# Splitting and turning the normalised attention output: GpSimd and DMA transposes in place of TensorE, ScalarE and VectorE

## What is computed

```python
x = x + tanh(g_xattn) * xattn(layernorm(x), ctx, Wq, Wk, Wv, Wo, bo)
x = x + tanh(g_ffn) * ffn(layernorm(x), gate_w, w_gate, w_up, w_down)

def xattn(x, context, Wq, Wk, Wv, Wo, bo):   # 16 heads of 16 channels
    q, k, v = x @ Wq.T, context @ Wk.T, context @ Wv.T          # split into heads
    scores = where(causal, einsum('bhqd,bhkd->bhqk', q, k) * 0.25, -inf)
    y = einsum('bhqk,bhkd->bhqd', softmax(scores), v)           # heads joined again
    return y @ Wo.T + bo

def ffn(x, ...):      # 8 experts, each takes the 128 tokens of a batch with the highest affinity
    affinity = softmax(x @ gate_w.T); gating, idx = top_k(affinity.T, 128)
    h = silu(x[idx] @ w_gate.T) * (x[idx] @ w_up.T)
    return scatter_add(idx, gating * (h @ w_down.T))
```

## Time and profile before

| | before |
|---|---|
| time of three runs, median (lowest to highest) | 2008.08 us (2006.38 to 2014.46) |
| the profiled execution: its own time; its span | 2008.71 us; 2006.9 us |
| busy share of the span: TensorE, VectorE, ScalarE, GpSimd | 92%, 56%, 45%, 35% |
| mean granted TensorE clock | 0.973 |
| attention, as a stretch of the trace | up to about 926 us |
| one body of attention in its steady part | 52.77 us |
| in such a body: TensorE, VectorE, ScalarE, GpSimd busy | 51.27, 42.32, 31.18, 22.55 us |

### The profile page before, as it was taken

The page is one execution under the profiler, slowest core; times in us unless marked ns, Lnnn a source line. Parts: engine busy times, 40 slices in busy tenths (PEclk is TensorE's granted clock), DMA queues, the critical chain, the costliest instruction groups (busy, mean ns, idle before and its releaser), DMA issues.

```text
span 2006.9 us, 41634 instructions
## 1 busy us (share of the span) xinstructions
PE 1847.0 (92%) x13800; PEld 1091.3 (54%) x13800; DVE 1122.4 (56%) x2745; ACT 898.1 (45%) x1716; POOL 709.5 (35%) x636
## 2 busy tenths in 40 slices
PE   3799999999999999992599999999999999999997
PEld 1455555555555555551256556565555656566565
DVE  3667787788887778766543443434333433434332
ACT  1355555555556555562243343433333333433332
POOL 4234444444444444223324233332424233342322
PEclk9799999999999999996799999999999999999999
DMA  4655565555555655526456454664545646444322
GB/s 128 147 143 144 162 166 154 155 149 161 156 161 161 167 158 163 132 82 154 132 103 125 81 98 85 115 122 85 99 81 95 122 74 120 94 73 90 58 28 26
DMA packets 378619, 238.32 MB, mean 119 GB/s; under 512 B 260600, under 2 KB 360064, under 8 KB 378496
## 3 DMA queue, kind: packets, MB, share of 16 engines
q1 hardware_dynamic: 353920, 203.14, 41.0%
q0 software_dynamic: 24576, 33.57, 10.6%
HBM read 118.63 MB, written 58.72 MB: 88 GB/s over the span
## 4 chain that ended last, share of the span: by engine, by line
PE 48%; DVE 2%; DMA 2%; issue 1%; POOL 0%; ACT 0%; DVEq 0%; POOLq 0%
PE bank L1037 11%; PE bank L1038 10%; PE bank L1039 10%; PE bank L1055 5%; PE bank L1053 5%; PE bank L1054 5%; DMA out<-y,row_now 1%; DVE top_at L1106 1%; DVE work L1109 1%; DVE top L1104 1%; POOL out L997 0%; DVE h L1144 0%; DMA tokT<-rows 0%; ACT y L1091 0%; POOL rows L989 0%
## 5 line engine op out<-in xcount | busy, mean ns | idle before, releaser
L558 ACT ACTIVATE prob<-bank 128x512 f32<-128x512 f32 x640 | 372.5, 597 | 221.6 <-PE bank L448 210.4
L997 POOL DMA_INDIRECT out<-y,row_now x128 | 201.6, 1575 | 661.4 <-ACT y L1091 637.1
L1144 DVE TENSOR_TENSOR h<-bank,silu 128x512 f32<-128x512 f32 x256 | 176.3, 689 | 341.4 <-PE bank L1039 340.4
L645 DVE CUSTOM_DVE_ANT_0 masked<-bank,causal 128x384 f32<-128x384 f32 (+1 forms) x512 | 299.3, 617 | 44.9 <-PE bank L428 44.1
L1083 ACT ACTIVATE h<-h 128x512 bf16<-128x512 f32 x256 | 161.1, 629 | 348.7 <-DVE h L1144 348.7
L428 PE MATMUL bank<-ks,qs 96*128 96x128 bf16 (+3 forms) x1024 | 277.8, 307 | 29.9 <-DMA ks<-k_parts 25.8
L1053 PE MATMUL bank<-downT,h 128*128 128x256 bf16 x1024 | 279.1, 273 | 0.0
L1054 PE MATMUL bank<-downT,h 128*128 128x256 bf16 x1024 | 279.1, 273 | 0.0
L1055 PE MATMUL bank<-downT,h 128*128 128x256 bf16 x1024 | 279.1, 273 | 0.0
L1147 DVE TENSOR_TENSOR h<-h 128x512 bf16<-128x512 f32 x256 | 177.2, 692 | 179.5 <-ACT h L1083 179.5
L446 PE MATMUL bank<-qs,ks 98*128 98x512 bf16 (+3 forms) x1024 | 268.4, 301 | 3.0 <-DMA qs<-m_sb 2.2
(11 more groups left out here) (144 smaller groups left out, 2784.0 us busy)
## 6 DMA issues: line engine op xcount, KB each, us to landing
qs<-q_parts SPq DMA_DIRECT2D x384, 64.0 KB, 2.7
ks<-k_parts SPq DMA_DIRECT2D x384, 64.0 KB, 2.7
q_parts<-q_sb SPq DMA_DIRECT2D x32, 384.0 KB, 3.1
k_parts<-k_sb SPq DMA_DIRECT2D x32, 384.0 KB, 3.2
x_t<-in_x SPq DMA_DIRECT2D x16, 512.0 KB, 4.1
ctx_t<-in_ctx SPq DMA_DIRECT2D x16, 512.0 KB, 4.9
res_t<-in_x SPq DMA_DIRECT2D x16, 512.0 KB, 5.6
out<-x SPq DMA_DIRECT2D x16, 512.0 KB, 3.0
```

The lines of the kernel that those rows point to most:

```text
L558: nc.scalar.activation(prob[:, gr % 2, h0:h0 + nh, POFF[tiles[0]]:POFF[tiles[0]] + w], sc_bank[SC_BANK[k]][:, 0:nh * w].rearrange("p (h w) ...
L645: nc.vector.tensor_tensor_reduce(masked[:, k % 2, 0:w], max_bank[max_at(gr, k)][:, 0:w], causal[:, T - w:T], 1.0, LOWEST, ALU.add, ALU.max ...
L997: nc.gpsimd.indirect_dma_start(out_rows, bass.IndirectOffsetOnAxis(ap=row_now[:, par, CHUNK * c + s:CHUNK * c + s + 1], axis=0), y[:, c % ...
```

## The change

`yb` and `yb+` go. Two new pieces take their place. `ysplit` (GpSimd) splits one half of `yq` into hi and lo in token layout, in the new tensor `y_nat`, with two instructions, at g1 k3 (half 0) and g3 k3 (half 1). `yturn` (SyncE) turns that half with one DMA transpose of 128x1024 bfloat16 into `ynT`, whose layout changes, at g1 k6 (half 0, first in its unit) and g3 k6 (half 1, ahead of `stack(b+1, 0)`). `o` waits for the transposes' semaphore. The job list has 20 entries a body instead of 22, so the alternation of banks is counted anew: `mt(b-1, 3)` (L469, g0 k4), which followed `yt(b-1, 0)` in one bank, now follows `v(b, 1)` of the body before.

```diff
         0: {...
-            2: [("yt+", b - 1, 0), ("yb", b - 2, 1), ("xsplit", b + 1, 1)],
-            3: [("pv", b - 1, 1, 2), ("mrow", b - 1, 3), ("yb+", b - 2, 1)],
+            2: [("yt+", b - 1, 0), ("xsplit", b + 1, 1)],
+            3: [("pv", b - 1, 1, 2), ("mrow", b - 1, 3)],
...
         1: {1: [("mt", b, 0)], 2: [("yt+", b - 1, 1)],
-            3: [("pv", b - 1, 2, 0), ("mt+", b, 0), ("ln2", b - 2, 0)],
+            3: [("pv", b - 1, 2, 0), ("mt+", b, 0), ("ln2", b - 2, 0), ("ysplit", b - 1, 0)],
...
-            6: [("q", b + 1, 1, 0), ("q", b + 1, 1, 1), ("q+", b + 1, 1)],
+            6: [("yturn", b - 1, 0), ("q", b + 1, 1, 0), ("q", b + 1, 1, 1), ("q+", b + 1, 1)],
...
         2: {...
-            3: [("yt", b - 1, 2), ("yb", b - 1, 0), ("yb+", b - 1, 0), ("k+", b + 1, 0)],
+            3: [("yt", b - 1, 2), ("k+", b + 1, 0)],
...
         3: {0: [("kstore", b + 1)], 1: [("mt", b, 2)],
-            2: [("mrow", b, 2), ("mt+", b, 2), ("yt", b - 1, 3), ("yt+", b - 1, 3)], 3: [("ll+", b - 2)],
+            2: [("mrow", b, 2), ("mt+", b, 2), ("yt", b - 1, 3), ("yt+", b - 1, 3)], 3: [("ll+", b - 2), ("ysplit", b - 1, 1)],
...
-            5: [("ln1", b + 2, 0)], 6: [("stack", b + 1, 0), ("lt", b - 2), ("lt+", b - 2), ("pv", b, 0, 1)],
+            5: [("ln1", b + 2, 0)], 6: [("yturn", b - 1, 1), ("stack", b + 1, 0), ("lt", b - 2), ("lt+", b - 2), ("pv", b, 0, 1)],
...
-JOBS_A_BATCH = {"yt": 4, "yb": 2, "o": 2, "mt": 4, "q": 2, "k": 2, "xt": 2, "ll": 1, "lt": 1, "v": 2}
+JOBS_A_BATCH = {"yt": 4, "o": 2, "mt": 4, "q": 2, "k": 2, "xt": 2, "ll": 1, "lt": 1, "v": 2}
...
-    ynT = sb(ctx, "ynT", [P, 2, NH2, T], BF16)
+    y_nat = sb(ctx, "y_nat", [P, NH2, 2, NT, P], BF16)
+    ynT = sb(ctx, "ynT", [P, NH2, 2, NT, P], BF16)
...
+                elif kind == "yturn":
+                    half = p[2]
+                    hold(split_lo["y"], count(b, 2, half + 1))
+
+                    hold(filled["o"], count(b, 2, 0))
+                    sp.dma_start_transpose(ynT[:, half, :, :, :].rearrange("p r i t -> p (r i) t"),
+                                           y_nat[:, half, :, :, :].rearrange("p r i d -> p (r i d)"))\
+                        .then_inc(flipped["y"], 16)
...
-                            wait(pe, read["yb"], count(b, 2, 2))
+                            wait(pe, flipped["y"], count(b, 32, 32))
...
-                        src = cT[:, rs, i, c, :] if kind == "v" else ynT[:, rs, c, i * P:(i + 1) * P]
+                        src = cT[:, rs, i, c, :] if kind == "v" else ynT[:, c, rs, i, :]
...
-                    wait(dve, filled["yb"], count(b, 2, gr // 2 - 1))
+                    wait(dve, split_lo["y"], count(b, 2, gr // 2 - 1))
...
+                elif kind == "ysplit":
+                    half = p[2]
+                    wait(pool, read["yt"], count(b, GROUPS, 2 * half + 2))
+
+                    wait_apart(pool, flipped["y"], count(b, 32, 16 * half - 16), passed["pool"])
+                    src = yq[:, :, half * P:(half + 1) * P]
+                    nc.gpsimd.tensor_copy(y_nat[:, half, 0, :, :], src).then_inc(split_hi["y"], 1)
+                    wait(pool, split_hi["y"], count(b, 2, half + 1))
+                    nc.gpsimd.tensor_tensor(out=y_nat[:, half, 1, :, :], in0=src, in1=y_nat[:, half, 0, :, :],
+                                            op=ALU.subtract).then_inc(split_lo["y"], 1)
```

More of the change, by code:

```diff
@@ L256, in attention @@
     read = {n: sem(f"{n}_read") for n in JOBS_A_BATCH}
-    hi_done = {n: sem(f"{n}_hi_done") for n in ("q", "k", "mt", "yb")}
+    hi_done = {n: sem(f"{n}_hi_done") for n in ("q", "k", "mt")}
     rest_split = sem("rest_split")
-    split_hi = {n: sem(f"{n}_hi_split") for n in ("x", "c")}
-    split_lo = {n: sem(f"{n}_lo_split") for n in ("x", "c")}
-    flipped = {n: sem(f"{n}_flipped") for n in ("x", "c")}
+    split_hi = {n: sem(f"{n}_hi_split") for n in ("x", "c", "y")}
+    split_lo = {n: sem(f"{n}_lo_split") for n in ("x", "c", "y")}
+    flipped = {n: sem(f"{n}_flipped") for n in ("x", "c", "y")}
     max_filled, max_read = sem("max_filled"), sem("max_read")
@@ L475, in piece @@
                     last.then_inc(filled[kind], 1)
-                elif kind in ("yb", "xt"):
+                elif kind == "xt":
                     half = p[2]
[L478 to L482, removed]
+                    wait(pe, ln_done["ln2"], count(b, NT, NT))
                     for i in range(NT):
-                        last = nc.tensor.transpose(to[:, i * P:(i + 1) * P], src[:, i, half * P:(half + 1) * P],
+                        last = nc.tensor.transpose(to[:, i * P:(i + 1) * P], xn2[:, i, half * P:(half + 1) * P],
                                                    ident[:, :])
@@ L573, in piece @@
                         .then_inc(hi_done["mt"], 1)
-                elif kind in ("yb+", "xt+"):
+                elif kind == "xt+":
                     half = p[2]
[L576 to L583, removed]
+                    wait(act, filled["xt"], count(b, 2, half + 1))
+                    wait(act, filled["ll"], count(b, 1, 0))
+                    nc.scalar.activation(xn2T[:, half, :], src[:, :], ACT.Copy).then_inc(read["xt"], 1)
                 elif kind in ("q+", "k+"):
@@ L656, in piece @@
                                                    ALU.mult, ALU.subtract).then_inc(read["mt"], 1)
[L657 to L662, removed]
                 elif kind in ("q+", "k+"):
```

## The result

The changed kernel takes 2075.43 us (median of 4, 2074.39 to 2079.65), the kernel before in the same session 2008.89 us: a ratio of 1.033 with a 95% interval of 1.0315 to 1.0351. It is slower by some 67 us, where I had forecast 47 to 48; the direction is right, the time lies 3 us above my range. The profiled execution took 2075.14 us, its span is 2073.3 us.

A forecast was written before the change was run, and what follows sets the result against it. TensorE's in-order stream was taken to bound a body. Losses of 39.2 (later stack), 22.4 (clock) and 3.5 us (end), less gains of 12.8 and 3.5, made +48.8 us on 2008.71; forecast 2056 us, range 2028 to 2072.

The forecast's parts named there:

- The step that read the load of group 0 as arriving last: At each body's start TensorE already waits 0.39 us for this load, so any delay on SyncE's queue costs one to one.
- what is gained: TensorE's removed transposes, 29 halves at 0.44 us, gain 12.8 us; L469's bank wait at g0 k4 gains 3.5 us.
- the clock: After the stall at a body's start TensorE runs at half clock: 1.6 us each, 14 times, 22.4 us lost.
- GpSimd's earlier work ends at 459.04, so it is just free: GpSimd can split half 1 about 0.1 us after yq is written at 459.15, so the split is ready at 461.1.
- the 2.8 us by which the stack starts later: On SyncE's queue the stack of group 0 starts at 463.15 instead of 460.35; 14 times, 39.2 us lost.
- the stack behind the x transposes shows nothing of that: Transposed data and loads hindering each other was priced at nothing; a further 1 us served only as upper bound.
- the end: In the last bodies the output projection starts 2.6 us later; with a lower clock for 24 matmuls, 3.5 us lost.
- Half 0: Its turn at g1 k6 costs nothing: the split is ready and the scores have about 1 us of cover.
- The case without the clock: Rival: TensorE waits 3.2 us at a body's start but the clock falls seldom, 2034 us; chance 0.22.
- that of the hidden split: Rival: GpSimd's split is done in time; only the transpose's 1.4 us issue delays the stack, clock stays up, 2015 us; chance 0.07.
- More than the stall: Rival: loads slowed a further 1 us, late row of maxima at g2, or clock staying down; 2070 us or above; chance 0.12.
- The faster case: Rival: group 0's load still lands with TensorE's arrival, the transpose leaving the queue before the row of maxima, 1995 us; chance 0.04.

The follow-up runs named there:

- experiment 1: Changed kernel with the turn of half 1 issued right behind the stack of group 0 instead of ahead of it: 2005.03 us, ratio 0.9969.
- experiment 10: Changed kernel with the turn of half 1 behind the stack of group 0 and the residual loaded ahead of x and the context: 1999.13 us, ratio 0.9954.
- experiment 6: Changed kernel with 14 useless 128x512 matmuls in front of TensorE's wait at a body's start: 2053.88 us, ratio 1.0212.
- experiments 2 and 8: 2: changed kernel, GpSimd's bias addition to the residual behind the split of half 1, 2064.58 us; 8: changed kernel, residual loaded ahead of x and context, 2060.75 us.
- experiment 5: Kernel before with one DMA transpose of 128x1024 zeros, read by nobody, ahead of the stack of group 0 in every body: 2045.42 us, ratio 1.0164.
- experiment 3: Changed kernel with the turn of half 0 moved from the first group to behind the residual's load (g2 k8): 2076.55 us, ratio 1.0333.
- experiment 4: Changed kernel where SyncE waits for the split of half 1 ahead of the stack of group 0 but issues the transpose behind it: 2048.88 us, ratio 1.0184.
- experiment 9: Changed kernel with only the wait for the split ahead of the stack, transpose behind it, and GpSimd splitting ahead of the residual's addition: 2030.33 us, ratio 1.0102.

## Why the prediction was right and wrong

**Right: what bounds, and where the loss arises.** The step that read the load of group 0 as arriving last, and concluded that whatever is put ahead of it is paid one to one, holds: 64.0 us of waits in 14 places, and moving the turn alone brings them back to 14.8 with all 14 starts counted (experiment 1).

**Right: what is gained.** I had 0.44 us for each half and the 3.5 us of L469's wait. The list of waits after has no wait for yq at that transpose any more. In experiment 10, where the stall is gone, bodies 5 to 14 last 51.36 us on the mean against 52.81 before, with the same waits at their starts within 0.05 us: 1.5 us less, against 2 x 0.44 + 0.39 = 1.3 by my terms. (The 390 ns of the Trainium skill, "VectorE: DVE Perf Modes", section "The three transpose paths", which the prediction sets beside this, is its figure for bfloat16; the transposes removed here are of float32.)

**Right in kind, and by luck in its sum: the clock.** 22.4 us forecast, 21.5 to 24 by experiment 6. But I had 1.6 us for each of 14 stalls, and the experiment shows 2.25 us for each of ten and leaves the other four open. I had taken a price near the shortest case in the trace of before; the granted clock fell short by 1.5 to 3.1 us.

**Wrong: the step "GpSimd's earlier work ends at 459.04, so it is just free", and with it the 2.8 us by which the stack starts later.** I took its time from the trace of before as if it stayed where it was. That addition waits for a DMA, and the change moves it against the rest: from the issue of the residual's load to the row of maxima it was 7.55 us before (451.15 to 458.70) and is 7.02 us after (541.47 to 548.49). I read this so: the chain of that load is anchored on the queue, the k products are anchored on TensorE, which had 0.44 us less to do in between, and ScalarE and VectorE a step less. No run tests that reading. With 0.2 us of later landing the split starts 0.6 us after yq instead of 0.1. In bodies 2 and 4 that load goes out only 5.7 and 4.8 us ahead of the row of maxima (7.3 us before), GpSimd waits 2.9 and 3.9 us for it, and the stalls are 8.2 and 7.4 us. So I had also priced 14 stalls from one steady body. Splitting first, or loading the residual first, takes 11 to 12 us of waits away, two thirds of them in the first four stalls (experiments 2 and 8).

**Wrong: "the stack behind the x transposes shows nothing of that".** I had put the hindrance between the transposed data and the loads at nothing and kept 1 us for the range. Over the 14 starts it is 0.52 us more from the last issue to TensorE's start, 7 us in all; with the transpose alone it is 0.36 us (experiment 5). The trace of before does show it, if all bodies are taken: in bodies 6 to 14 the last load of the stack behind the x transposes lands after 2.98 us, that of group 0 after 2.73.

Together these two are the mis-sized term: 2.8 us a stall, 39.2 us, where 53.5 us was measured (64.0 - 10.5): the first load 0.63 us later than forecast and 0.52 us of landing, less 0.13 us of shorter issues, 14 times. With my gains the sum is 53.5 + 21.5 of clock + 4.3 for the end (I had 3.5) - 16.3 = 63, against 66.4 us of difference between the two spans. It closes in bodies 5 to 14: 34.5 us more of waits + 22.5 of clock - 15.0 of gains = 42.0, where they last 41.7 us longer. What is left over lies in the bodies before and behind them, and no run assigns it.

**Half 0.** I had its turn at nothing. No wait for the row of maxima appeared at g2 k0, so its cover held. With it moved, the stalls at bodies 2 and 4 are 2.7 and 1.1 us shorter and the time is the same; whether it pushes the residual's load in the steady bodies stays open (experiment 3).

**The rivals.** The case without the clock is refuted by experiment 6, that of the hidden split by experiment 4: the wait for the split is the larger part. *More than the stall* came nearest in time, but none of its three causes is the late split: the loads land half a microsecond later, not one; the row of maxima at g2 is in time; the clock falls short by 2.5 us a stall on the mean. The faster case asked rightly for a first load that goes out on time, but I saw only one way to it, a transpose issued ahead of the row of maxima. In another kernel than the one forecast the turn stands one place further down, in a gap of the queue of 1.7 us (in the trace of before the stack of group 0 ends at 465.87, the next starts at 467.54).

## What to carry to other kernels

An in-order DMA queue is an engine like the others: before a transfer is put into it, find the transfer behind it that already arrives last, and put the new one after it, into a gap. The DMA transpose, with the wait for its data, cost 70 us of run time ahead of one load, compared with its place behind it, where the steady starts wait 0.7 us instead of 0.6 in the kernel before. And where a cost is "the engine is just free by then", ask what its earlier work waits for: a wait on a transfer does not move along when the compute engines get faster, so the slack has to be computed for the changed order. One steady body is not enough for that: the first bodies, where transfers land later, held more than a third of the waits here.

## What the runs showed of the hardware

In the changed kernel a DMA transpose of 128x1024 bfloat16 holds the issuing queue for 1.23 to 1.34 us, more than three plain DMAs of 64 KB (0.37 us each), and lands 3.15 us after its issue. Of the 12 plain loads behind the one of experiment 5 the first ten land within 0.1 us of their old delay, the last 0.4 us later.

TensorE's clock can fall after idle times hardly longer than the 1.59 us that left it alone in the trace of before, and not in each case; the prediction took a stall of 1.8 us as one that leaves the clock up. In experiment 9, where stalls differ little, one of 1.78 us was followed by half clock and one of 1.99 us was not:

```profile
369.51 0.23 PE L439 MATMUL bank<-ks,qs 96*128 96x128 bf16 x1 [1.78 <-DMA ks<-k_parts]
...
586.75 0.23 PE L439 MATMUL bank<-ks,qs 96*128 96x128 bf16 x1 [1.99 <-DMA ks<-k_parts]
```

```profile
371.00:372.00 1.00, 1.00 (x8) 0.00 (x0) 0.67 (x2) 0.38 (x1) 0.08 (x1) 0.50 0.44 131
...
588.00:589.00 1.00, 1.00 (x13) 0.39 (x6) 0.76 (x3) 0.29 (x1) 0.00 (x0) 1.00 0.50 131
```

In the changed kernel, with stalls of 3.4 us and more, the clock was down after each of the 14. Useless matmuls in the stall kept it up and made the kernel 1% faster while it computed more.
